# A three-layer image network on one core: attention in units of three heads, the router and one normalisation by token halves

## The reference

```
x = x + conv(group_norm(x))      # row and column recurrences, a gate per token, LayerNorm over channels
t = tokens(x)                    # 1024 tokens of 192 channels per image
t = t + attention(layer_norm(t)) # 6 heads of 32; every token sees 33 neighbours and token 0; token 0 sees all
t = t + experts(layer_norm(t))   # router: softmax over 4 experts, best 2, weights made to sum to 1;
                                 # each expert: 192 -> 768, GELU, 768 -> 192
x = from_tokens(t)
```

## Time and profile before

| what | value |
|---|---|
| time, median of 3 runs (lowest, highest) | 3024.24 us (3016.46, 3027.24) |
| the profiled execution: its own time, its span | 3024.18 us, 3022.4 us |
| mean granted TensorE clock | 0.884 |
| busy: PE, PEld | 2486.9 us (82%), 1970.4 us (65%) |
| busy: DVE, ACT, POOL | 1944.9 us (64%), 1047.9 us (35%), 936.1 us (31%) |
| products without a reader (L1594) | 462, 126.8 us |
| exponentials of the router (L743) | 16, 86.8 us |

### The profile page before, as it was taken

How to read it: one execution, slowest core, us unless ns; L and a number is a source line. 1 busy time by engine, 2 the same in 40 slices (tenths; PEclk the granted TensorE clock), 3 DMA queues, 4 the chain that set the end, 5 groups by cost and what they waited for, 6 DMA issues and landing times. The chain is left out here.

```text
span 3022.4 us, 52214 instructions
## 1 busy us (share of the span) xinstructions
PE 2486.9 (82%) x18977; PEld 1970.4 (65%) x18977; DVE 1944.9 (64%) x5732; ACT 1047.9 (35%) x2533; POOL 936.1 (31%) x704
## 2 busy tenths in 40 slices
PE   1368686988988898888889898988889898989597
PEld 0256575766777676666767676766677676767365
DVE  4456465676767666676767666766767676766364
ACT  0032333334242434334242524343342524343122
POOL 0000304033242505143242515151332425051644
PEclk9777787799989889999999999899989989899799
DMA  1650322427272533527272615435262725344565
GB/s 43 117 161 21 84 56 73 104 67 166 68 175 68 133 84 93 123 72 160 67 175 68 165 54 134 107 89 127 69 162 68 175 68 143 73 109 117 144 161 107
DMA packets 373055, 320.88 MB, mean 106 GB/s; under 512 B 209244, under 2 KB 350782, under 8 KB 362176
## 3 DMA queue, kind: packets, MB, share of 16 engines
q1 hardware_dynamic: 312064, 226.15, 29.0%
q0 software_dynamic: 50880, 52.59, 10.0%
q10 hardware_dynamic: 9856, 38.80, 4.0%
HBM read 182.53 MB, written 107.52 MB: 96 GB/s over the span
## 5 line engine op out<-in xcount | busy, mean ns | idle before, releaser
L1558 PE MATMUL PSUM<-XT,WB 128*128 128x512 f16 x2010 | 534.1, 401 | 27.1 <-DMA META<-slots 26.2
L861 ACT ACTIVATE HF<-PSUM,WB 128x512 f32<-128x512 f32 x402 | 274.7, 687 | 613.0 <-PE PSUM L1558 605.6
L884 ACT ACTIVATE PSPT<-PSUM,NMX 94x126 f32<-94x126 f32 x1056 | 286.8, 362 | 473.3 <-DVE NMX L1157 321.4
L1576 PE MATMUL PSUM<-WB,HHI 128*128 128x192 f16 x1608 | 411.2, 256 | 0.2
L1577 PE MATMUL PSUM<-WB,HHI 128*128 128x192 f16 x1608 | 410.3, 255 | 0.0
L1578 PE MATMUL PSUM<-WB,HLO 128*128 128x192 f16 x1608 | 409.8, 255 | 0.0
L768 POOL DMA_INDIRECT out_dram<-Y,META x228 | 368.9, 1618 | 129.3 <-issue 129.3
L720 POOL TENSOR_TENSOR TR<-TV,MHALF 128x4 f32<-128x4 f32 x64 | 75.5, 1180 | 1025.1 <-DVE TV L975 1025.1
L1103 DVE TENSOR_SCALAR HHI<-HF 128x512 f16<-128x512 f32 x402 | 177.0, 440 | 289.4 <-ACT HF L861 286.2
L1558 PEld LDWEIGHTS PSUM<-XT,WB 128*128 128x128 f16 x2010 | 202.7, 105 | 202.1 <-issue 42.3
L1633 PEld LDWEIGHTS PSUM<-VW,PSPT 126*94 126x94 f32 x2112 | 240.8, 196 | 137.9 <-DVE PSPT L1141 135.6
(11 more groups left out here) (274 smaller groups left out, 4703.2 us busy)
## 6 DMA issues: line engine op xcount, KB each, us to landing
WB<-weights SPq DMA_DIRECT2D x67, 1600.0 KB, 7.3
KST<-heads SPq DMA_DIRECT2D x96, 189.0 KB, 4.6
QST<-heads SPq DMA_DIRECT2D x96, 141.0 KB, 3.6
XR<-in_x ACTq DMA_DIRECT2D x16, 768.0 KB, 7.9
out_dram<-X ACTq DMA_DIRECT2D x32, 384.0 KB, 2.6
heads<-QT SPq DMA_DIRECT2D x32, 282.0 KB, 2.7
KST<-heads SPq DMA_DIRECT2D x48, 141.8 KB
weights<-WB ACTq DMA_DIRECT2D x4, 1600.0 KB, 6.8
```

Source lines behind the costliest of these rows:

```text
L861: act.activation(HF[:, k % 2, :], PSUM[:, 4 + k % 2, :], ACT.Gelu, scale=1 / (X_UP * W_UP), bias=bias).then_inc(f["gelu_done"], 1)
L884: e = act.activation(PS[0:QS, n % 2, h, :], PSUM[0:QS, n % 2, h * KS:(h + 1) * KS], ACT.Exp, bias=NMX[:, b, n % 2, h:h + 1])
L1558: mm = pe.matmul(dst, WB[:, ws, w:w + 128], XT[:, xs, chunk, :], start=(n == 0), stop=(n == 4))
L1576: pe.matmul(dst, HHI[:, k % 3, tok], w2h, start=False, stop=False, skip_group_check=True)
```

## The change

It has three parts.

1. **Attention** goes by units of three heads. In turn n (of 25) TensorE makes the scores of unit n, the transposes of unit n-2 and the value products of unit n-3; VectorE takes the maximum of unit n, copies the transposes of unit n-2 and, at odd n from 5, normalises block (n-5)/2. Scores rotate over three banks (0, 1, 5) instead of two, value products lie in banks 6 and 7 by turns, so `turn` no longer waits for a normalisation and `values` waits for that of two blocks before. The 28 products without a reader are gone. The next image's norm pieces stand at the same place by unit number: statistics after units 2 and 4, spread 8, variance 12, image 16 and 18.
2. **Router.** The power is split by token halves, the later half (computed first) ahead of the mixing LayerNorm's root on GpSimd, the other behind it. `gates` runs once for each half, at dispatch steps 20 and 26; each pass has all 15 instructions, on half the width.
3. **First LayerNorm, second half.** ScalarE's four activations and GpSimd's shift are gone; VectorE normalises the four tiles itself (`norm_tokens`) inside `first_halves`, straight behind GpSimd's root.

The diff, cut to its core:

```diff
 # VectorE, attention
-                    o = PSUM[0:QS, 2, O_COL:O_COL + HEADS * VC].rearrange("p (h d) -> p h d", h=HEADS)
+                    o = PSUM[0:QS, 6 + b % 2, 0:HEADS * VC].rearrange("p (h d) -> p h d", h=HEADS)
...
-                for b in range(NB + 1):
...
+                for n in range(UNITS + 4):
+                    if n < UNITS:
+                        dve.wait_ge(s["score_done"], at("score_done", i, n + 1))
+                        dve.tensor_reduce(NMX[:, n // 2, n % 2, :],
+                                          PSUM[0:QS, SCORE_BANK[n % 3], 0:HH * KS].rearrange("p (h k) -> p h k", h=HH),
+                                          AX.X, ALU.max, negate=True).then_inc(s["max_done"], 1)
+                    if 2 <= n < UNITS + 2:
+                        copy_turned(n - 2)
+                    if n >= 5 and n % 2 == 1:
+                        normalize((n - 5) // 2)
...
+                        if n in (2, 4):
+                            norm_channels(i + 1, n // 2 - 1)
+                        if n == 8:
+                            norm_spread(i + 1)
+                        if n == 12:
+                            norm_variance(i + 1)
+                        if n in (16, 18):
+                            norm_image(i + 1, (n - 16) // 2)
 # TensorE, attention
-                    if n >= 2:
-                        pe.wait_ge(s["exp_done"], at("exp_done", i, n - 1))
+                    if n >= 3:
+                        pe.wait_ge(s["exp_done"], at("exp_done", i, n - 2))
...
-                        pe.wait_ge(s["o_normed"], at("o_normed", i, n // 2))
...
+                    if oh == 0 and b >= 2:
+                        pe.wait_ge(s["o_normed"], at("o_normed", i, b - 1))
...
-                        keep_busy(8 if b == 1 else 2)
...
+                for n in range(UNITS + 3):
+                    if n < UNITS:
+                        scores(n)
+                    if 2 <= n < UNITS + 2:
+                        turn(n - 2)
+                    if n >= 3:
+                        values(n - 3)
 # GpSimd
                     conv_states(i + 1)
+                route_exp(i, 1)
+                if not last(i):
                     rstd(i + 1, GTR[:], GTV[:], NT, "mixln_eps", "mixln_rstd")
-                route_exp(i + 1)
+                route_exp(i, 0)
 # ScalarE
                     if t == 6:
-                        first_norm(i, 0)
-                yield from til(step_no, 36)
-                first_norm(i, 1)
+                        first_norm(i)
 # VectorE
-                dve.wait_ge(s["xn1_ready"], at("xn1_ready", i, k + 1))
+                    dve.wait_ge(s["xn1_ready"], at("xn1_ready", i, 1))
+                else:
+                    dve.wait_ge(s["ln1_rstd"], at("ln1_rstd", i, 2))
+                    link(norm_tokens(X1, range(4, 8)))
...
+                yield from til(step_no, 20)
+                gates(i, 1)
                 yield from til(step_no, 26)
-                gates(i)
+                gates(i, 0)
```

More of the change, by code:

```diff
@@ L548, in evacuate_v @@
                               ).then_inc(s["piece_dve"], 1)
-        O_COL = HH * QS
+        UNITS, SCORE_BANK = 2 * NB, (0, 1, 5)
         CLS_COL = 480
@@ L888, in attention, with first_norm @@
                 act.activation(CW[:], CW[:], ACT.Exp).then_inc(s["cls_exp"], 1)
-            def first_norm(i, k):
-                act.wait_ge(s["ln1_shift"], at("ln1_shift", i, k + 1))
-                for t in range(4 * k, 4 * k + 4):
+            def first_norm(i):
+                act.wait_ge(s["ln1_shift"], at("ln1_shift", i, 1))
+                for t in range(4):
                     a = act.activation(XN[:, t, 0:C], X1[:, t, :], ACT.Identity, bias=NMR[:, t:t + 1],
@@ L1261, in route, with gates @@
                 dve.tensor_tensor(SC[:, tiles], SC[:, tiles], sm, ALU.subtract).then_inc(s["route_shift"], 1)
-            def gates(i):
-                se, sm1, win = SE[:], SM[:], WIN[:]
-                sm = sm1.unsqueeze(2).broadcast_to((128, NT, E))
-                dve.wait_ge(s["route_exp"], at("route_exp", i, 0))
+            def gates(i, half):
+                tiles = slice(4 * half, 4 * half + 4)
+                se, sm1, win, cmpa, cmpb = SE[:, tiles], SM[:, tiles], WIN[:, tiles], CMPA[:, tiles], CMPB[:, tiles]
+                sm = sm1.unsqueeze(2).broadcast_to((128, 4, E))
+                dve.wait_ge(s["route_exp"], at("route_exp", i, -half))
                 link(dve.tensor_reduce(sm1, se, AX.X, ALU.add))
@@ L1270, in gates @@
                 link(dve.tensor_tensor(se, se, sm, ALU.mult))
[L1271 to L1280 removed]
+                mine = se.unsqueeze(3).broadcast_to((128, 4, E, E))
+                other = se.unsqueeze(2).broadcast_to((128, 4, E, E))
+                dve.tensor_tensor(cmpa, mine, other, ALU.is_ge)
+                link(dve.tensor_tensor(cmpb, mine, other, ALU.is_gt))
+                dve.tensor_tensor(cmpa, cmpa, AFTER[:].unsqueeze(1).broadcast_to((128, 4, E, E)), ALU.mult)
+                link(dve.tensor_tensor(cmpb, cmpb, BEFORE[:].unsqueeze(1).broadcast_to((128, 4, E, E)),
+                                       ALU.mult))
+                link(dve.tensor_tensor(cmpa, cmpa, cmpb, ALU.add))
+                link(dve.tensor_reduce(win, cmpa, AX.X, ALU.add))
+                w = dve.tensor_scalar(WINB[:, tiles], win, 2.0, None, ALU.is_ge)
+                if half == 0:
+                    w.then_inc(s["winners"], 1)
                 link(dve.scalar_tensor_tensor(win, win, 2.0, se, ALU.is_ge, ALU.mult))
@@ L1284, in gates @@
                 link(dve.reciprocal(sm1, sm1))
-                dve.scalar_tensor_tensor(GATE, win, 1 / (W_UP * H_UP), sm, ALU.mult, ALU.mult)
+                dve.scalar_tensor_tensor(GATE[:, tiles], win, 1 / (W_UP * H_UP), sm, ALU.mult, ALU.mult)
             def positions(i):
@@ L1636, in values @@
                         mm.then_inc(s["pv_done"], 1)
-                for b in range(NB + 1):
-                    if b < NB:
-                        scores(2 * b)
-                        scores(2 * b + 1)
-                    if b >= 1:
-                        turn(2 * b - 2)
-                        turn(2 * b - 1)
-                        keep_busy(8 if b == 1 else 2)
-                        values(2 * b - 2)
-                        values(2 * b - 1)
-                    if following and b == 3:
+                for n in range(UNITS + 3):
[5 more added lines that the diff above has]
+                        values(n - 3)
+                    if following and n == 6:
                         group_mean(i + 1)
-                    if following and b == 5:
+                    if following and n == 10:
                         group_variance(i + 1)
```

57 lines of the change are left out of this document (18 added, 39 removed).

## The result

The changed kernel takes 2768.02 us (median of 4 runs, 2759.76 to 2782.22) against 3021.31 us before: a ratio of 0.917, 95% interval 0.912 to 0.921. The profiled execution is the slowest of the four, 2782.22 us with a span of 2780.4, 242 us less than the profiled one of before. Of that, the sixteen attentions have 194.0 and the fifteen stretches between them 43.2.

What follows compares the result with a forecast made beforehand. In attention VectorE was taken to bound at the full clock, TensorE at the lower. From 3024 us, attention took off 139 and the expert stage 45, giving 2840 us; range 2745 to 2935.

Steps and rivals of the forecast that it cites:

- What bounds an attention: Attention: VectorE bounds at the full clock, 31 us; TensorE at the lower, 43.5 us, a lost level not returning.
- How many keep it: Attention: half of images 3 to 14 keep the full clock, images 0 to 2 slow; sum 608 against 747, -139 us.
- nearly all hold: Rival in attention: units close the gaps, twelve images at 31 us, -216 us, total 2763; chance 0.23.
- the likeliest case: Attention: half hold, 4 to 8 of twelve images keep the full clock, about 2800 to 2880 us; chance 0.42.
- (a): Attention: dropping the products without a reader saves 0.32 us of TensorE's work per block at full clock, 0.63 at the lower.
- all fall: Rival in attention: the opening loses the level in every attention, -64 us, total 2915; all or most fall, chance 0.27.
- Router: Expert stage: half-width power of 3.1 us and a 2.95 us pass gain 1.5 us per image, bounds -1.4 and +2.9.
- First normalisation: Expert stage: VectorE normalising the second half cuts TensorE's 3.36 us wait by 1.5 us per image, bounds 0 and 3.36.
- The experts' sum: Expert stage: router and first LayerNorm, 1.5 us each in fifteen images, -45 us, bounds -94 and +21.
- The slower rivals: Behind attention: the lower clock outlasts attention into output projection and first expert chunks, 3078 us; slower, chance 0.03.
- The last rival: Attention's waits only change semaphores, 41 to 45 us at full level; step 20 eats the router's part; about 3010; chance 0.05.

Runs made afterwards that it cites:

- the run with attention alone: The kernel before with only the attention part of the change (units of three heads, no products without a reader): 2799.28 us, executions from 2747.52 to 2824.17.
- the ground of products: The changed kernel with its 28-odd products without a reader put back: 2683.81 us; without the router's part 2735.04, without the normalisation's 2692.42, without both 2742.08.
- the run with the statistics' gaps: The changed kernel with four products without a reader in each of the two gaps of the channel statistics, none in the first gap: 2719.30 us.

## Why the prediction was right, and where it was not

**What bounds an attention: right.** I took 31 us at the full level, from VectorE's own work, and 43.5 at the lower one, from TensorE's; it is 30.3 and 44.4. VectorE is busy for 96% of the first, and a block of the second takes 3.97 us where I had 4.03. That a level once lost does not return was right for the three attentions that lost it inside and for images 1 and 2, which started low, and wrong for image 0, which started low and was back at 1.00 by 218. Image 15, 27 if it held, took 26.4.

**How many keep it: the step that failed.** I took six of images 3 to 14, from a busy share of 56% against 59%, and all of images 0 to 2 as slow. Nine of the twelve held, and image 0: attention gave 194 us where I had 139, and the result lies on the side of the rival "nearly all hold", 2763, to which I gave 0.23, not of the likeliest case with 0.42. That it still lies in my range, 23 us above its lower end, is owed to the width of the range and not to this step. The share was no measure to decide by. The windows of the openings of image 12 (first three) and image 13 (last three), at equal distances from the first maximum, begin with the same work, and one of them falls:

```profile
2014.30:2016.70 2.40, 0.97 (x11) 0.75 (x10) 1.86 (x6) 1.82 (x8) 1.99 (x2) 1.00 1.04 253
2016.70:2018.70 2.00, 1.38 (x16) 1.16 (x15) 2.00 (x6) 0.84 (x5) 1.54 (x1) 1.00 1.09 235
2018.70:2020.70 2.00, 1.90 (x23) 1.83 (x24) 2.00 (x5) 1.41 (x6) 1.55 (x1) 1.00 1.12 277
2161.60:2164.00 2.40, 0.97 (x10) 0.79 (x10) 1.86 (x6) 1.86 (x8) 1.96 (x2) 1.00 0.96 212
2164.00:2166.00 2.00, 1.72 (x16) 1.39 (x15) 2.00 (x6) 0.84 (x5) 1.55 (x1) 0.70 1.07 230
2166.00:2168.00 2.00, 1.93 (x12) 1.82 (x13) 2.00 (x5) 1.38 (x6) 1.54 (x1) 0.50 1.17 267
```

Up to the fall no row tells the two apart: TensorE's and VectorE's instructions stand at the same distances from the first maximum: the first transposes 1.49 us behind it in both, each after a wait of 1.43 us, the first statistics 2.35 and 2.36 us, the first value products 2.54 and 2.55. The Trainium skill (TensorE: Matmul & The Clock Gate, Part 1, "What's actually happening") says that the activity is counted in a window that runs free of the program; that would make like openings fall or not by chance of time, as they do here, and as the spread of the run with attention alone suggests. No run here shows it directly. Images 0 to 2 are another matter: I took them as slow for their low clocks before, and what made them start low, TensorE's wait for the heads, stood in no term of mine.

**Dropping the products: the wrong sign.** Under (a) I priced it as work saved. At the lower level a block is 0.69 us shorter (3.97 against 4.66; I had 0.63), but without the products that level lasts: with them back the kernel is 84 us faster. The rule that speaks against this part stood in the prediction as the rival "all fall", with 0.27; it was right on the mechanism and not on the size, since in units eleven of the sixteen attentions held the level, or came back to it, without the products. In the old order it would have been right altogether, 866.3 us with every attention down.

**Router: right in its working, short in its price.** The rows that answer to the earlier trace rows:

```profile
1202.77 2.90 POOL L746 TENSOR_TENSOR SE<-EBASE,SC 128x16 f32<-128x16 f32 x1 [5.84 <-DVE SC L1269]
...
1205.71 0.17 DVE L1277 TENSOR_REDUCE SM<-SE 128x4 f32<-128x16 f32 x1 [1.71 <-POOL SE L746]
...
1208.53 0.17 DVE L1296 SCALAR_TENSOR_TENSOR XROW<-WIN,SM 128x16 f32<-128x16 f32 x1
...
1211.37 0.26 PE L1503 MATMUL PSUM<-ROWS,ONES 128*128 128x192 bf16 x1 [2.65 <-DVE X L1069]
```

The half power takes 2.90 us (I had 3.1), VectorE waits 1.71 us for it instead of 3.02, and the pass lasts from 1205.71 to 1208.70, 2.99 us (2.95). TensorE's wait went from 4.53 to 2.65, 1.9 instead of 1.5; over the whole trace such waits went from 74.7 to 44.5 us. The new pass at step 20 waits for nothing: of the 32 passes 16 wait. What I did not price is the clock: on the ground of products TensorE's busy time, with the same instructions, is nearly half of the part's worth. The lower bound that I gave the step, -1.4, comes out at -1.3 from its own terms; the sum does not hang on it.

**First normalisation: the wait went, the time hardly.** The rows that answer to the earlier trace rows:

```profile
1230.67 1.24 DVE L990 TENSOR_SCALAR XN<-X,TMV,TR 128x192 f32<-128x192 f32 x4
...
1233.64 0.83 PE L1520 MATMUL PSUM<-EYEH,X 128*128 128x128 f16 x12 [1.90 <-DVE X L1198]
...
1239.18 0.20 DVE L501 COPY OSX<-PSUM 128x11 f16<-128x11 f16 x1
...
1239.48 1.47 PE L1546 MATMUL PSUM<-OSX,WQKV 128*96 128x372 f16 x5 [1.94 <-issue]
```

The wait ahead of the second set of transposes (L1520, before L1509) went from 3.36 to 1.90 us, 1.46 where I had 1.5. But a new wait of 1.94 us stands at the projections (L1546). The profile names no releaser for it; they wait for the windows that ScalarE and VectorE copy, and VectorE's last copy (L501) ends 0.1 us ahead of them, behind the engine's own row of work, to which the change added 1.24 us. On the ground of products that wait was 0.37 us without this part and 1.95 with it; over the whole trace the waits ahead of the transposes went from 65.2 to 45.4 us and this one from 4.1 to 25.8, and TensorE's idle time between attentions was 155.2 us without the part (1719.6 - 1564.4) and 155.5 with it. The gain was given back one step later; I had looked for what was late next on ScalarE and not on VectorE.

**The experts' sum was near for a reason that I had only half.** I had 45 us from less waiting; it is 43.2, of which 35.7 are idle time, most of it the router's, and 7.5 TensorE's busy time, which is the clock. That these two parts are worth 56 us with products in attention and next to nothing here beyond attention's own effect (1756.7 with attention alone, 1750.3 with all) says that in the change as it stands the clock takes back what they save: TensorE's busy time there is 1597.3 us, with attention alone 1568.9. The part of this that the runs locate is the first 4 us behind an attention, where the clock is down behind all twelve of images 3 to 14 in the change and behind three with attention alone; why is not shown.

**The slower rivals** did not come: behind the fallen attentions of images 3, 13 and 14 the stretches take 116.6, 119.8 and 119.8 us, as behind the others (116.6 to 120.0), and no wait at step 20 appeared. The last rival's sum, 3024 - 20, is 3004 and not about 3010.

## What to carry to other kernels

Price an instruction that computes nothing by the clock it keeps, in its own stage and in the next, before pricing it by its length. Where a stage has two levels of speed, ask of each gap which of them it risks, and fill the first gap and the end of the stage first: here 28 short products, 16 in the opening and 12 at the end, brought some 98 us on a kernel of 2768. A wait taken off one engine's row is worth what the next wait on that row leaves of it; look along the row of the engine that took over the work.

## What the runs showed of the hardware

GpSimd's power goes nearly by width: 128 by 4 in 1.2 to 1.3 us, 128 by 16 in 2.9, 128 by 32 in 5.4, so that two halves cost 0.4 us more than the whole. TensorE at 1.2 GHz can be busy without a gap, with transposes and products that fill part of its 128 rows and columns, and stay there for the rest of an attention (changed kernel, image 13, busy for all of 2168 to 2182 at 0.50; so in images 3 and 14). With four products that fill all of 128 by 128, over 378 columns, near the fall it was back within 5 us (the windows of image 14 in the run with the statistics' gaps; so in all five falls of that run). In image 13 a busy share of 100%, by the profile's count, did not bring the level back; what it is about the four products that does, no run here separates.
